# Two square roots in the first steps of a hyperbolic attention, and top-1 experts that scatter finished rows

## The reference

```
diff_sq = max(|q|^2 + |k|^2 - 2 q.k, 0)
denom = max((1 - |q|^2)(1 - |k|^2), 1e-6)
distance = arccosh(max(1 + 2 diff_sq / denom, 1))
out = softmax(-distance) @ v
```

```
xf = layernorm(x)
e = argmax(xf @ Wg + bg)              # one of 8 experts for each token
out = x + gelu(xf @ W1[e]) @ W2[e]
```

## Time and profile before

| | us |
|---|---|
| median of 3 runs | 1285.22 (1282.93 to 1285.47) |
| profiled execution, its own time | 1284.13 |
| its span, first to last instruction | 1281.7 |
| busy in the span: DVE / PE / ACT / POOL | 973.9 / 947.0 / 765.2 / 571.5 |
| hyperbolic attention | 603 to 1127 |
| top-1 experts, routing / expert stage | 1183 to 1210 / 1210 to 1282 |

### The profile page before, as it was taken

The page is one execution under the profiler, slowest core; times in us unless marked ns, Lnnn a source line. Parts: engine busy times, 40 slices in busy tenths (PEclk is TensorE's granted clock), DMA queues, the critical chain, the costliest instruction groups (busy, mean ns, idle before and its releaser), DMA issues. The chain is left out here.

```text
span 1281.7 us, 16656 instructions
## 1 busy us (share of the span) xinstructions
PE 947.0 (74%) x5186; PEld 464.4 (36%) x5186; DVE 973.9 (76%) x2104; ACT 765.2 (60%) x995; POOL 571.5 (45%) x490
## 2 busy tenths in 40 slices
PE   5886955799997449992766788877888887445294
PEld 2553342455554339991300011111111111034294
DVE  5676678688883557775799999999899999756532
ACT  3303666266665314441625999999999999821041
POOL 0004100022221037651456888888888878200174
PEclk9997986599999559996855555566555556565598
DMA  6000001231100137762251000010000000020164
GB/s 189 15 1 1 0 1 42 67 87 57 45 26 2 58 122 237 237 200 84 82 161 49 25 24 25 29 43 26 25 25 25 25 25 1 1 68 27 54 175 133
DMA packets 61015, 80.70 MB, mean 63 GB/s; under 512 B 15049, under 2 KB 38012, under 8 KB 60672
## 3 DMA queue, kind: packets, MB, share of 16 engines
q1 hardware_dynamic: 51936, 67.85, 17.6%
q0 software_dynamic: 3968, 8.13, 2.0%
q10 hardware_dynamic: 5024, 3.67, 0.9%
HBM read 64.09 MB, written 15.34 MB: 62 GB/s over the span
## 5 line engine op out<-in xcount | busy, mean ns | idle before, releaser
L2813 POOL TENSOR_TENSOR hb_t<-hb_t,hb_r 128x512 f32<-128x512 f32 x248 | 362.3, 1501 | 69.2 <-ACT hb_r L2623 67.7
L2826 DVE TENSOR_SCALAR hb_dpos<-hb_psR 128x1024 f32<-128x1024 f32 x128 | 155.6, 1216 | 23.1 <-PE hb_psR L2548 18.4
L2572 PE MATMUL hb_psO<-hb_t,ha_va 128*9 128x512 f32 x512 | 113.6, 987 | 59.3 <-ACT hb_t L2652 55.1
L2557 PE MATMUL hb_psR<-ha_q,ha_k 20*128 20x512 bf16 x256 | 127.1, 596 | 40.8 <-DVE hb_dpos L2826 40.8
L2834 DVE SCALAR_TENSOR_TENSOR hb_t<-hb_psR,hb_dpos 128x1024 f32<-128x1024 f32 x128 | 154.9, 1210 | 0.0
L2149 ACT ACTIVATE ga_att<-ga_psB 128x512 f32<-128x512 f32 (+3 forms) x256 | 100.8, 453 | 67.7 <-PE ga_psB L2075 47.8
L2548 PE MATMUL hb_psR<-ha_q,ha_k 78*128 78x512 bf16 x256 | 128.0, 603 | 7.8 <-DMA ha_k<-hsx 3.5
L2170 DVE TENSOR_REDUCE ga_nm<-ga_psA 128x1 f32<-128x128 f32 (+3 forms) x256 | 113.0, 484 | 21.8 <-PE ga_psA L2053 20.4
L2652 ACT ACTIVATE hb_t<-hb_t 128x4096 f32<-128x4096 f32 (+2 forms) x32 | 111.2, 3522 | 0.0
L2843 DVE SCALAR_TENSOR_TENSOR hb_r<-hb_t 128x1024 f32<-128x1024 f32 x64 | 106.0, 1656 | 0.0
L2020 POOL TENSOR_SCALAR_AFFINE_SELECT ga_att<-ga_att 128x512 f32<-128x512 f32 x48 | 30.6, 637 | 133.8 <-ACT ga_att L2149 133.8
(11 more groups left out here) (477 smaller groups left out, 2088.9 us busy)
## 6 DMA issues: line engine op xcount, KB each, us to landing
m2x_e_w<-in_L_ffn_W_dram SPq DMA_DIRECT2D x78, 256.0 KB
m1x_e_w<-in_L_ffn_W_dram SPq DMA_DIRECT2D x23, 256.0 KB
ga_q<-qx SPq DMA_DIRECT2D x48, 96.0 KB
ha_q<-hqx SPq DMA_DIRECT2D x48, 96.0 KB
ha_k<-hkx SPq DMA_DIRECT2D x48, 96.0 KB
hy_fwd<-in_const_fwd_dram SPq DMA_DIRECT2D x1, 2048.0 KB
f_down<-in_L_ffn_W_dram ACTq DMA_DIRECT2D x4, 512.0 KB, 4.4
hsx<-hp_aparts SPq DMA_DIRECT2D x6, 288.0 KB
```

Source lines behind the costliest of these rows:

```text
L2557: mm = pe.matmul(psR[:, side_slot(n), i, :], k[SIDE:SIDE + SROWS, it % 2, i0 + i, P * c:P * c + P], q[SIDE:SIDE + SROWS, it % 2, i0 + i, : ...
L2572: mm = pe.matmul(psO[32 * i:32 * i + VW, :], va[:, CH * (it // G) + c, HPG * (it % G) + i, :], t[:, (2 * it + form) % T_QUADS, 2 * half + ...
L2813: half_sum = pool.tensor_tensor(tt, tt, rr, ALU.add)
L2826: dve.tensor_scalar(dpos[:, n % 2, :], psR[:, dist_slot(n), :, :].rearrange("p i t -> p (i t)"), 0.0, None, ALU.max).then_inc(dpos_ready, 1)
```

## The change

In hyperbolic attention, steps 0 to 2 use the two roots for both quads; from step 3 on nothing changes in the forms. ACT's order at the start is written out anew: both quads of step 0 and the first of step 1 have their roots before the first logs, the second quad of step 1 follows with step 2. The preload in the pass without roots is gone. `inverses(1)` stands at n = 2. In the top-1 experts a row of `m1x_tokens` holds the normed token and the residual side by side (1 KB), one gather brings both, DVE adds the residual where it copied, and POOL scatters the finished rows into the output itself; slots without a token get a row number beyond the output, which is skipped. Ring XR is 8, a load waits until the output of the tile 8 before is written by DVE, and a store stands directly behind the load. The read back, the last sum and the last store are gone. The top-2 experts keep the old way.

```diff
@@ Experts.__init__
+        self.direct = top == 1
+        self.RW = 2 * D if self.direct else D
-        self.tokens = nc.dram_tensor(name + "_tokens", [TOKENS, D], F32).ap()
+        self.tokens = nc.dram_tensor(name + "_tokens", [TOKENS, self.RW], F32).ap()
@@ mixture, routing stage
-                    sp.dma_start(ex.tokens.rearrange("(p g) d -> p g d", p=P), tok[:, :, :]).then_inc(kept, 16)
+                    rows = ex.tokens.rearrange("(p g) d -> p g d", p=P)
+                    sp.dma_start(rows[:, :, 0:D], tok[:, :, :]).then_inc(kept, 16)
+                    if direct:
+                        sp.dma_start(rows[:, :, D:RW], x[:, :, :]).then_inc(kept, 16)
...
+                    if direct:
+                        ch.tick(dve.scalar_tensor_tensor(out=line[:, :], in0=tile_of, scalar=float(P), in1=later[:, :], op0=ALU.mult, op1=ALU.add))
...
+                    if direct:
+                        ch.tick(dve.scalar_tensor_tensor(out=spare[:, :], in0=line[:, :], scalar=-1.0, in1=spare[:, :], op0=ALU.add, op1=ALU.add))
@@ mixture, expert stage
-            XR, WR, YR, DR = 6, 4, 4, 3
+            XR, WR, YR, DR = 8 if direct else 6, 4, 4, 3
-            xt = s.sb("xt", [P, XR, D])
+            xt = s.sb("xt", [P, XR, RW])
...
-                    fetch(sp, 0)
-                    if out is not None:
-                        for q in range(TILES // 4):
-                            sp.wait_ge(summed, q + 1)
-                            sp.dma_start(out[q].rearrange("(c p) d -> p c d", p=P), x[:, 4 * q:4 * q + 4, :]).then_inc(out_stored, 16)
-                        sp.wait_ge(out_stored, 16 * (TILES // 4))
+                    if not direct:
+                        fetch(sp, 0)
...
-                        if t >= XR:
+                        if t >= XR and direct:
+                            pool.wait_ge(y_ready, t - XR + 1)
+                        elif t >= XR:
                             pool.wait_ge(x_turned, t - XR + 1)
...
+                        if direct:
+                            pool.indirect_dma_start(out=out.rearrange("b t d -> (b t) d"), out_offset=where, in_=yo[:, t % YR, :], in_offset=None,
+                                                    bounds_check=TOKENS - 1, oob_is_err=False).then_inc(stored[t % YR], 16)
...
-                        if t >= 3:
+                        if direct:
+                            store(t)
+                        elif t >= 3:
                             store(t - 3)
...
-                            dve.tensor_copy(yo[:, t % YR, :], psY[:, t % 2, 0:D]).then_inc(y_ready, 1)
+                            dve.tensor_tensor(yo[:, t % YR, :], psY[:, t % 2, 0:D], xt[:, t % XR, D:RW], ALU.add).then_inc(y_ready, 1)
...
-                        if top == 1:
-                            quad = x[:, 4 * q:4 * q + 4, :]
-                            dve.tensor_tensor(quad, quad, got[:, 0, 4 * q:4 * q + 4, :], ALU.add).then_inc(summed, 1)
@@ hyperbolic_attention
+            PLAIN = 3
+            def by_product(it, form):
+                return form == 0 and it >= PLAIN
@@ ScalarE
                     def product_roots(it):
-                        act.wait_ge(m_ready, QUAD * (it + 1))
+                        act.wait_ge(m_ready, QUAD * (it - PLAIN + 1))
...
-                    def two_roots(it):
-                        act.wait_ge(t_ready, UNITS * (it + 1))
-                        if it >= 1:
-                            act.wait_ge(sum_ready, 2 * (UNITS * (it - 1) + QUAD))
-                        act.activation(quad(r, it, 1), quad(t, it, 1), ACT.Sqrt)
-                        act.activation(quad(t, it, 1), quad(t, it, 1), ACT.Sqrt, bias=one[:, 0:1]).then_inc(root_ready, 1)
+                    def two_roots(it, form):
+                        act.wait_ge(t_ready, max(n for n in range(UNITS * it, UNITS * it + UNITS) if place(n)[1] == form) + 1)
+                        if 2 * it + form >= R_QUADS:
+                            act.wait_ge(sum_ready, 2 * QUAD * (2 * it + form - R_QUADS + 1))
+                        act.activation(quad(r, it, form), quad(t, it, form), ACT.Sqrt)
+                        act.activation(quad(t, it, form), quad(t, it, form), ACT.Sqrt, bias=one[:, 0:1]).then_inc(root_ready, 1)
+                    def roots(it, form):
+                        if by_product(it, form):
+                            product_roots(it)
+                        else:
+                            two_roots(it, form)
...
-                    for it in range(STEPS + 3):
+                    roots(0, 0)
+                    roots(0, 1)
+                    roots(1, 0)
+                    act.preload_act_table_set("natural_log_exp_and_others")
+                    logs(0, 0)
+                    logs(0, 1)
+                    weights(0, 0)
+                    weights(0, 1)
+                    roots(1, 1)
+                    for it in range(2, STEPS + 3):
                         if it < STEPS:
-                            product_roots(it)
-                            two_roots(it)
-                        if 1 <= it < STEPS + 1:
+                            roots(it, 0)
+                            roots(it, 1)
                             act.preload_act_table_set("natural_log_exp_and_others")
+                        if it < STEPS + 1:
                             logs(it - 1, 0)
...
@@ VectorE
-                        if n == 4:
+                        if n == 2:
                             inverses(1)
...
-                        if 2 <= n <= TOTAL + 1 and place(n - 2)[1] == 0:
+                        if 2 <= n <= TOTAL + 1 and by_product(*place(n - 2)[0:2]):
                             product(n - 2)
```

More of the change, by code:

```diff
@@ L1584, in store @@
                         pool.wait_ge(y_ready, t + 1)
-                        pool.indirect_dma_start(out=ex.outputs, out_offset=bass.IndirectOffsetOnAxis(ap=target[:, t:t + 1], axis=0),
-                                                in_=yo[:, t % YR, :], in_offset=None).then_inc(stored[t % YR], 16)
+                        where = bass.IndirectOffsetOnAxis(ap=target[:, t:t + 1], axis=0)
+                        if direct:
+                            pool.indirect_dma_start(out=out.rearrange("b t d -> (b t) d"), out_offset=where, in_=yo[:, t % YR, :], in_offset=None,
+                                                    bounds_check=TOKENS - 1, oob_is_err=False).then_inc(stored[t % YR], 16)
+                        else:
+                            pool.indirect_dma_start(out=ex.outputs, out_offset=where, in_=yo[:, t % YR, :], in_offset=None).then_inc(stored[t % YR], 16)
                     for t in range(XR):
@@ L1592, in _ @@
                             load(t + XR)
-                        if t >= 3:
+                        if direct:
+                            store(t)
+                        elif t >= 3:
                             store(t - 3)
-                    for t in range(NT - 3, NT):
-                        store(t)
+                    if not direct:
+                        for t in range(NT - 3, NT):
+                            store(t)
                     for n in range(YR):
@@ L1606, in turn_tokens @@
                             pe.wait_ge(xT_ready, t - 1)
-                        pe.transpose(psX[:, t % 2, 0:P], xt[:, t % XR, :], ident[:, :]).then_inc(x_turned, 1)
+                        pe.transpose(psX[:, t % 2, 0:P], xt[:, t % XR, 0:D], ident[:, :]).then_inc(x_turned, 1)
                     def first_products(t):
@@ L1673, in _ @@
                             tokens(t + 3)
-                    fetch(act, 1)
+                    if not direct:
+                        fetch(act, 1)
                 @block.vector
@@ L1722, in _ @@
                     output(NT - 1)
+                    if direct:
+                        return
                     ch = Chain(dve, comb_done)
@@ L1728, in _ @@
                         dve.wait_ge(arrived[q], 16 * top)
-                        if top == 1:
-                            quad = x[:, 4 * q:4 * q + 4, :]
-                            dve.tensor_tensor(quad, quad, got[:, 0, 4 * q:4 * q + 4, :], ALU.add).then_inc(summed, 1)
[L1732 to L1735, removed]
-                                                                     in1=x[:, g, :], op0=ALU.mult, op1=ALU.add))
-                                ch.join()
+                        for k in range(top):
+                            for g in range(4 * q, 4 * q + 4):
+                                ch.tick(dve.scalar_tensor_tensor(out=x[:, g, :], in0=got[:, k, g, :], scalar=prob[:, k, g:g + 1],
+                                                                 in1=x[:, g, :], op0=ALU.mult, op1=ALU.add))
+                            ch.join()
 def mixture_top2(nc, A, ex, x, xn, ident):
@@ L2643, in logs @@
                             act.wait_ge(sum_ready, 2 * (UNITS * it + QUAD * (form + 1)))
-                        if form == 1:
+                        if by_product(it, form):
```

(6 more changed lines are left out.)

20 lines of the change are left out of this document (10 added, 10 removed).

## The result

The changed kernel takes 1276.69 us (median of 5 runs, 1276.08 to 1279.16), the one before 1285.22 beside it (5 runs, 1282.93 to 1286.54). The ratio is 0.9941 with a 95% interval of 0.9925 to 0.9957: 7.6 us less, between 5.5 and 9.6 (the two medians alone differ by 8.5). The prediction was 1273.3, inside 1270 to 1276 if the forecast held and inside 1269.5 to 1279.5 in eight cases of ten. The profiled execution of after is one of 1276.69 us with a span of 1274.2 us, against 1284.13 and 1281.7 before.

A forecast was written before the change was run, and what follows sets the result against it. ACT was taken to bound the loop and POOL's queue the expert stage. Gains of 5.2 and 6.7 us made 11.9, so 1272.2 us profiled, 1273.3 as median; own range 1270 to 1276, eight in ten 1269.5 to 1279.5.

The forecast's parts named there:

- rival (b): Loop: gives nothing, as units come slower or a supplier slips a little each step; 1278.5 us, chance 0.12.
- rival (a): Experts: wide gathers land late beside weight loads, 2 to 4 us more; 1275.3 to 1277.3 us, chance 0.13.
- When ACT can start, how much it waits: Loop's start: first root 6.6 us earlier, 8.6 us less idle, three roots 10.7 us more; 5.0 us gained.
- 6.6 us earlier: Loop's start: ACT's first root at 656.0 instead of 662.65, with inverses moved ahead and products of units 0 to 3 gone.
- DVE saves 12 products, but that is off the path: Loop's start: the products DVE saves, 1.13 us each, were counted as no gain on the path.
- The loop's end: Loop's end: dropping the 1.28 us preload gains only 0.2 us (bounds 0 and 1.3), as DVE's chain is late next.
- The routing stage: Before the experts: the second 1 MB write is hidden with 14 us of cover; one added DVE instruction costs 0.1 us.
- Two gathers fewer ahead, wide rows, the addition: Experts: 37 intervals, 48.05 us, last store 2.6 us later; wide gathers 0.5 us; addition costs DVE the same as the copy.
- The bounds check: Expert stores: 0 to 0.1 us a store on POOL's queue, taken as 0.
- Rival (c): Expert gathers: POOL's descriptor writing grows with a row's bytes, 1.94 us a load instead of 0.97; 1293 us, chance 0.07.
- The tail: Experts' end: last store lands 2.24 us after its start, then 0.6 us to the end; end at 1275.0 against 1281.7.
- The sum: Whole kernel: 5.2 + 6.7 = 11.9 us off the profiled 1284.13, giving 1272.2; 1273.3 against the median of three.

The follow-up runs named there:

- `PLAIN` 2: Changed kernel with two roots in steps 0 and 1 only, not 0 to 2 (value 3): median 1273.05 us of 6 runs, one at 1289.91.
- narrow rows: Changed kernel storing and gathering only the token's 512 bytes; the output adds the token, the residual is left out: 1275.67 us (4 runs).
- the variant with the fastest runs here: Changed kernel with two roots in steps 0 and 1 only, ten gather buffers, final waits on SP: four of 12 runs 1269.0 to 1269.7, eight 1281.9 to 1287.2.

## Why the prediction came out as it did

The direction was right; the likeliest time was 3.4 us too low. The measured 1276.69 lies in the range of eight in ten but above the forecast's own 1270 to 1276. That it fell inside the wider range is partly luck: that range was drawn wide to take in rival (b), and the time even falls where rival (a) put it (1275.3 to 1277.3), while neither rival came true and what added the time, the DRAIN, was in no term.

- **When ACT can start, how much it waits.** Right in size: first root 14.69 us behind the first clipped unit (14.64 predicted; the rows added up without rounding give about 15.0), waits 3.00 and 7.59 (3.2 and 7.7), lead 5.02 (5.0). Rival (b) is out. But the sum named its parts wrongly. Of the "6.6 us earlier" the inverses' move is no cause: with them back at unit 4 the lead is the same. Only the last wait decides, the one for unit 13, and for that the inverses cost DVE the same on either side. And "DVE saves 12 products, but that is off the path" is wrong for the four of step 1: put back, they hold the root of step 1 up by 7.2 us. Only the four of step 2 are off the path; the third step of two roots bought nothing with them and cost a root of 3.5 us, so the same loop with `PLAIN` 2 leads by 8.5 us and not 5.0.
- **The loop's end.** 0.2 us predicted, 0.0 found. It was DVE's chain. The first gather came 563.99 us from the first clipped unit and not 569.34, 5.35 less: 0.33 more than the lead, and between 5.35 and 6.0 in the nine traces with the new loop and `PLAIN` 3. PE's last values took 3.52 us, at a mean granted clock of 0.77, instead of the 4.14 of the earlier trace rows at 0.66 (0.50 and 1.00 are the two levels). They take 3.1 to 3.5 us in the ten traces with the new loop and no long product, and 4.0 to 4.3 in the four others; why is open. The routing stage, from POOL's DRAIN at its start to the first gather, took 28.06 us and not 27.56: 0.5 us more, where 0.1 was predicted.
- **Two gathers fewer ahead, wide rows, the addition.** Predicted 61.5 us from the first gather to the last store, found 61.18. But two misses cancel in it. The queue resumes after the first output at 12.71 us from the first gather, where 12.84 and the wide row's 0.5 were counted: 0.6 us sooner. The wide row does cost its 0.5, 0.6 by the narrow rows' trace; but that trace resumes at 12.02, against 12.84 and 12.74 in the two traces with the old experts, so something else in the change brings the first output forward by 0.7 to 0.8 us; two gathers fewer ahead of it may do so, which no run isolates. From there the 37 intervals take 48.47 us and not 48.05. The bounds check was taken at 0; the store's median is 1.014 us where it was 0.990, 0.5 us over 23, though its target changed too and no run parts the two. (An estimate from the slope in the Trainium skill, DMA: Bandwidth & Descriptors, Anatomy of one DMA, is 0.15 us for the wide row, which the spread of 0.1 to 1.0 does not exclude.) What rival (a) feared did not come: the known landings are 3.0 to 4.6 us (that "all 23 loads" landed in 2.7 to 4.1 before was read from four known ones). Rival (c) is out by the gather's 975 ns.
- **The tail.** This step failed: "Last store starts at ... 1272.2, lands 2.24 us later ... From there to the end ... I take 0.6." The landing took 2.1 us, but behind it stand 4.4 us: POOL's DRAIN of 3.81 and the meeting of the queues. From the last store's start to the end 2.84 us were predicted and 6.48 measured, 3.64 more. The 0.6 came from the end of before, where SP ended last and its DRAIN is 7 ns. I took it over to a stage that ends on POOL. The cover that hid the DRAIN was the very read back that the change removes, and DRAINs stand in no list of busy time; the line view of the block had it at 1271.6.
- **The sum.** Against the predicted 1272.2 the profiled execution has 1276.69: 3.64 for the tail and 1.21 for the later first clipped unit (that beginning moves between traces of one and the same code ahead of it), less 0.36 for the rest.

## What to carry over

When a change takes away the last work of a stage, look at what every queue does at the block's end, the unbusy instructions too, and ask which of them was hidden by the work that goes; a queue that issued indirect DMAs ends late. A gain ahead of a wait counts only if it moves the last wait. And a shorter path on one engine can close the pauses of another on which a third seems to rely: take more than a few runs before believing a median, since the variant with the fastest runs here lands at 1269 or at 1285 us by chance.

## What the runs showed of the hardware

- POOL's DRAIN at a block's end costs 81 to 82 ns for each indirect DMA issued since its last DRAIN (38: 3160 ns, 46: 3809, 78: 6425), with gathers of 512 or 1024 bytes a row (3806 and 3809 ns), and can run while the last DMA is landing. The one set right behind eight fresh gathers ended 0.4 us after the last of them had landed.
- An indirect gather of 128 rows holds POOL's queue for 0.97 us with 512 bytes a row and for 0.98 with 1024; its landing, from issue, has a median of 3.5 and 3.2 us narrow (before, narrow rows) and 3.5 wide: the bytes hardly show.
- A DVE instruction with both inputs in SBUF, 1.2 to 2.3 us elsewhere, took 19.4 and 21.0 us while POOL's additions followed one another without a pause, and came through a us after they ended; a third trace with the same 40 additions has it at 1.43 us.
